# An adaptive-norm block on one core: the first tile's path to its first product, and the order around the fourth feed

## The reference, cut to what matters

```
u_m = u * mask                                # u: 64 x 64 x 1024, mask: position < length of the batch row
kernel[h, l] = 2 Re sum_n Cs[h, n] exp(dtA[h, n] * l)      # 64 heads h, 64 complex states n
y = causal_convolution(u_m, kernel) + u_m * D;  y = y * mask
scores = y @ Wr.T                             # 64 experts
gates = softmax(top 16 of scores), zero elsewhere
out = 2 * sum_k gates[k] * (y @ A[k].T) @ B[k].T           # rank 16 each
result = x + out
```

## Time and profile before

| | |
|---|---|
| median of 3 runs | 902.21 us (902.03 to 902.34) |
| the profiled execution | 900.6 us, its span 898.8 us |
| TensorE busy | 883.5 us, 98% of the span |
| VectorE busy | 764.9 us, 85% |
| ScalarE busy | 386.3 us, 43% |
| granted TensorE clock | 1.00 |

### The profile page before, as it was taken

How to read it: one execution, slowest core, us unless ns; L and a number is a source line. 1 busy time by engine, 2 the same in 40 slices (tenths; PEclk the granted TensorE clock), 3 DMA queues, 4 the chain that set the end, 5 groups by cost and what they waited for, 6 DMA issues and landing times.

```text
span 898.8 us, 15709 instructions
## 1 busy us (share of the span) xinstructions
PE 883.5 (98%) x4509; PEld 787.3 (88%) x4509; DVE 764.9 (85%) x2557; ACT 386.3 (43%) x682; POOL 2.0 (0%) x12
## 2 busy tenths in 40 slices
PE   5999999999999999999999999999999999999998
PEld 4667998998899998889998889998889999889997
DVE  8899989888898888898888898888888888888722
ACT  4763554344443354443344443344444344442100
POOL 0000000000000000000000000000000000000000
PEclk9999999999999999999999999999999999999999
DMA  6621214443434444434544333444433444344331
GB/s 221 253 58 47 77 30 135 112 125 105 116 103 111 125 120 105 109 105 106 134 111 111 107 112 96 134 111 111 109 120 100 120 111 113 109 123 107 99 94 47
DMA packets 67123, 99.85 MB, mean 111 GB/s; under 512 B 22944, under 2 KB 49184, under 8 KB 67104
## 3 DMA queue, kind: packets, MB, share of 16 engines
q1 hardware_dynamic: 66400, 99.16, 40.6%
q10 hardware_dynamic: 704, 0.46, 0.2%
HBM read 60.52 MB, written 34.87 MB: 106 GB/s over the span
## 4 chain that ended last, share of the span: by engine, by line
PE 93%; DVE 5%; ACT 1%; DMA 0%; issue 0%; ACTq 0%; DVEq 0%
PE out_ps L1286 25%; PE h_ps L1286 18%; PE out_ps L1290 12%; PE h_ps L1290 9%; PE turn_ps L1286 8%; PE turn_ps L1290 4%; PE conv_ps L1243 2%; PE conv_ps L1244 1%; PE conv_ps L1242 1%; PE conv_ps L1225 1%; PE conv_ps L1226 1%; PE conv_ps L1252 1%; PE conv_ps L1227 1%; PE conv_ps L1253 1%; PE conv_ps L1254 1%; PE h_ps L1295 1%
## 5 line engine op out<-in xcount | busy, mean ns | idle before, releaser
L1286 PE MATMUL out_ps<-b_lo,g_hi 128*128 128x512 f32 x496 | 195.3, 394 | 0.0
L1286 PE MATMUL out_ps<-b_hi,g_hi 128*128 128x512 f32 x496 | 195.2, 394 | 0.0
L1286 PE MATMUL h_ps<-a_hi,y_hi 128*128 128x384 f32 x480 | 161.4, 336 | 0.0
L1286 PE MATMUL h_ps<-a_lo,y_hi 128*128 128x384 f32 x480 | 161.3, 336 | 0.0
L1290 PE MATMUL out_ps<-b_hi,g_lo 128*128 128x512 f32 x496 | 122.9, 390 | 0.0
L1290 PEld LDWEIGHTS out_ps<-b_hi,g_lo 128*128 128x128 f32 x496 | 93.1, 188 | 20.3
L1286 PEld LDWEIGHTS out_ps<-b_hi,g_hi 128*128 128x128 f32 x496 | 93.1, 188 | 19.8
L1286 PEld LDWEIGHTS out_ps<-b_lo,g_hi 128*128 128x128 f32 x496 | 93.2, 188 | 19.5
L751 DVE SCALAR_TENSOR_TENSOR z<-swapped,step_other,part 128x64 f32<-128x64 f32 x384 | 92.3, 282 | 11.9
L744 DVE SCALAR_TENSOR_TENSOR part<-z,step_own,conv_ps 128x64 f32<-128x64 f32 x384 | 90.5, 277 | 8.5
L1290 PE MATMUL h_ps<-a_hi,y_lo 128*128 128x384 f32 x480 | 93.1, 336 | 0.0
(11 more groups left out here) (225 smaller groups left out, 1512.1 us busy)
## 6 DMA issues: line engine op xcount, KB each, us to landing
xt_in<-in_xt SPq DMA_DIRECT2D x32, 512.0 KB, 3.2
x_in<-in_x SPq DMA_DIRECT2D x62, 256.0 KB, 3.6
out<-x_in SPq DMA_DIRECT2D x62, 256.0 KB, 3.1
moved<-square_sb SPq DMA_DIRECT2D x28, 512.0 KB, 2.6
square_sb<-moved SPq DMA_DIRECT2D x112, 128.0 KB, 2.9
b_in<-in_b_t SPq DMA_DIRECT2D x8, 512.0 KB, 6.4
a_in<-in_a_t SPq DMA_DIRECT2D x8, 512.0 KB, 7.7
t_lo<-k_sb SPq DMA_DIRECT2D x62, 64.0 KB, 4.1
```

The source lines that it names most:

```text
L1286: pe.matmul(o, hi[:, c, :], moving[:, c, columns], start=first and c == order[0] and moving is w_hi, stop=False)
```

## The change

On the first tile:
- The parameters arrive by four transfers of 32 partitions (two per queue) instead of eight of 16. The first early block of B is loaded ahead of x, and ScalarE rounds it before its tanh instead of after the phases.
- `arguments(0)` moves ahead of the last weight operations. Two small operations make `weigh`, the real partitions' alpha and beta of the two heads.
- The kernel row comes straight from the powers: per head two products, with a column of `weigh` read 128 times (step 0) as weights. `out_factors(0)` goes behind `add_skip(0)`.
- TensorE starts with `whole_b(0)`, then 8 idle products instead of 14, then the row, and no longer waits for the rates. ScalarE's `low_weights(0)` stands ahead of `sines(0)`, and `copy_k(0)` ahead of `whole_in(0)`.
- The eight transfers of the block go out head by head with a semaphore for each. Near products run head by head; chunk 0 goes to a bank of its own and is masked alone, ahead of the third state step, then chunks 1 to 3 together. The mask itself is made in two halves, between the shuffle and the second part of two state steps. The from-states products of the upper chunks come before chunk 3's product with A instead of chunk 2's.

In the fourth iteration (t = 3) ScalarE takes the high part of the fed powers ahead of the y copies, and VectorE both `low_in` and `low_x` ahead of `low_row`.

```
-            for quad in range(P // QUAD):
-                first = quad * QUAD
-                sp.dma_start(par[first:first + PAIR, :, :], parameters[quad * PAIR:(quad + 1) * PAIR, :, :])...
-            sp.dma_start(xt_in[:, :, :], xt[0, :, :]).then_inc(s_xt, 16)
-            for i in EARLY:
-                load_weights(i)
+            for quad in (0, 1):
+                sp.dma_start(par[quad * QUAD:(quad + 1) * QUAD, :, :], states_of(quad)).then_inc(s_par, 16)
+            load_weights(EARLY[0])
+            sp.dma_start(xt_in[:, :, :], xt[0, :, :]).then_inc(s_xt, 16)
+            load_weights(EARLY[1])
...
-            for block, source in first_rows(0):
-                sp.dma_start(block, source).then_inc(s_t0, 16)
+            for i in range(HT):
+                for block, source in first_rows(i, range(0, JM // 2)):
+                    sp.dma_start(block, source).then_inc(s_t0[i], 16)
...      # ScalarE, start
+            split_weights(EARLY[0])
             act.wait_ge(s_rates, 1)
             act.activation(tanh_half[:, :], rates[:, :], ACT.Tanh, scale=0.5).then_inc(s_tanh, 1)
...
-            split_weights(EARLY[0])
+            low_weights(0)
             sines(0)
             split_weights(EARLY[1])
+            copy_k(0)
             whole_in(0, in_ps)
-            copy_k(0)
...      # ScalarE, step
+                second = isinstance(t, int) and t == LAGGED
                 if prep:
                     high_out(t + 2)
+                if second:
+                    high_in(t + 2)
                 if conv:
                     for i in range(HT):
                         high_y(t + 1, i)
                 if prep:
                     high_x(t + 2)
-                    if isinstance(t, int) and t == LAGGED:
-                        high_in(t + 2)
-                    else:
+                    if not second:
                         high_moved_in(t + 2)
...      # VectorE, start
+            arguments(0)
             dve.scalar_tensor_tensor(out=re_im, ...)
...
+            dve.tensor_scalar(weigh[:, 0, :], alpha[:, 0:HT], real_only[:, :], None, ALU.mult).then_inc(s_weigh, 1)
+            dve.tensor_scalar(weigh[:, 1, :], beta[:, 0:HT], real_only[:, :], None, ALU.mult).then_inc(s_weigh, 1)
             make_powers(0)
-            out_factors(0)
...
             add_skip(0)
+            out_factors(0)
...
-            states(0, range(1, 3))
-            ...                       # len_f and the whole mask
-            states(0, range(3, 4))
-            mask_first(0)
+            states(0, range(1, 2), lambda: mask_of(0, NC // 2))
+            states(0, range(2, 3), lambda: mask_of(NC // 2, NC))
+            dve.wait_ge(s_near0, 1)
+            dve.wait_ge(s_mask, 2)
+            mask_chunks(0, 1, s_ym0)
+            states(0, range(3, 4))
+            dve.wait_ge(s_conv0, HT)
+            mask_chunks(1, NC // 2, s_ym0)
             states(0, range(4, FED))
             arguments(1)
-            mask_first(1)
+            mask_chunks(NC // 2, NC, s_ym)
...      # VectorE, step
                 if prep:
                     low_out(t + 2)
+                    if second:
+                        low_in(t + 2)
+                        low_x(t + 2)
                     low_row(t + 2)
...
-                if prep:
+                if prep and not second:
                     low_x(t + 2)
-                    if second:
-                        low_in(t + 2)
-                    else:
-                        low_moved_in(t + 2)
+                    low_moved_in(t + 2)
...      # TensorE
+            def weighed_row():
+                pe.wait_ge(s_weigh, 2)
+                pe.wait_ge(s_powers, 1)
+                for i in range(HT):
+                    for part in range(2):
+                        last = pe.matmul(k_ps[:, i, :], weigh[:, part, i:i + 1].to_broadcast([P, P]), powers[:, i, part, 0:P], ...)
+                last.then_inc(s_kps, 1)
...
-            pe.wait_ge(s_rates, 1)
-            for n in range(14):
-                pe.matmul(turn_ps[:, 0, 0:P], ident[:, :], ident[:, :], start=True, stop=True)
             whole_b(0)
+            for n in range(8):
+                pe.matmul(h_ps[:, 0, 0:P], ident[:, :], ident[:, :], start=True, stop=True)
+            weighed_row()
             turn_in(0)
-            whole_row(0, k_ps)
             whole_feed(0)
-            pe.wait_ge(s_kcopy, 1)
             whole_b(1)
-            pe.wait_ge(s_t0, HT * JM * 16)
-            whole_near_0(0)
+            pe.wait_ge(s_blo, 2)
+            pe.wait_ge(s_t0[0], JM * 16)
+            whole_near_0(0, 0, 1)
+            whole_near_0(0, 1, NC // 2)
+            whole_near_0(0, NC // 2, NC)
+            pe.wait_ge(s_t0[1], JM * 16)
+            whole_near_0(1, 0, 1).then_inc(s_near0, 1)
+            whole_near_0(1, 1, NC // 2)
             whole_from_states_0(0)
-            whole_near_0(1).then_inc(s_near, 1)
+            whole_near_0(1, NC // 2, NC).then_inc(s_near, 1)
```

More of the change, by code:

```diff
@@ L475, in _ @@
             act.wait_ge(s_kdone, 1)
-            for block, source in first_rows(1):
-                act.dma_start(block, source).then_inc(s_t0, 16)
-            low_weights(0)
+            for i in range(HT):
+                for block, source in first_rows(i, range(JM // 2, JM)):
+                    act.dma_start(block, source).then_inc(s_t0[i], 16)
             theta(1)
@@ L734, in first_states, with mask_of, states @@
                 dve.wait_ge(s_first, HT * t + HT)
-            def states(t, chunks):
+            def mask_of(first, end):
+                dve.wait_ge(s_mask, 1)
+                dve.tensor_tensor(out=mask[:, first:end, :], in0=pos_f[:, first:end].unsqueeze(2).to_broadcast([P, end - first, B]),
+                                  in1=len_f[:, :].unsqueeze(1).to_broadcast([P, end - first, B]), op=ALU.is_lt).then_inc(s_mask, 1)
+            def states(t, chunks, amid=None):
                 n, moves = HT * t, FED - 1
@@ L1227, in feed @@
                     pe.matmul(fed, in_lo[:, i, :], xt_hi[:, i, 0:NS], start=False, stop=True).then_inc(s_fed, 1)
+            def weighed_row():
+                pe.wait_ge(s_weigh, 2)
+                pe.wait_ge(s_powers, 1)
+                for i in range(HT):
+                    for part in range(2):
+                        last = pe.matmul(k_ps[:, i, :], weigh[:, part, i:i + 1].to_broadcast([P, P]), powers[:, i, part, 0:P],
+                                         start=part == 0, stop=part == 1)
+                last.then_inc(s_kps, 1)
             def whole_feed(t, heads=range(HT)):
@@ L1254, in from_states, with whole_near_0 @@
                     pe.matmul(later, o_lo[:, i, 1:P + 1], z_hi[:, :, i, :], start=False, stop=True).then_inc(s_conv, 1)
-            def whole_near_0(n):
-                columns = slice(n * HALF // 2, (n + 1) * HALF // 2)
-                for i in range(HT):
-                    last = pe.matmul(conv_0[n][:, i, :, :], t_lo[:, i, :].bitcast(F32), xt_in[:, i, columns],
-                                     start=i == 0, stop=False, skip_group_check=True)
-                return last
+            def whole_near_0(i, first, end):
+                n = first // (NC // 2)
+                target = first_conv[:, i, :] if end == 1 else conv_0[n][:, i, first - n * (NC // 2):end - n * (NC // 2), :]
+                return pe.matmul(target, t_lo[:, i, :].bitcast(F32), xt_in[:, i, first * B:end * B],
+                                 start=i == 0, stop=end == 1 and i == HT - 1, skip_group_check=True)
             def whole_from_states_0(n):
```

55 lines of the change are left out of this document (30 added, 25 removed).

## The result

| | before | after |
|---|---|---|
| median | 902.12 us (900.73 to 902.34, 4 runs) | 912.43 us (911.07 to 913.26, 4 runs) |
| ratio | | 1.0121, 95% interval 1.0109 to 1.0132 |
| profiled execution, its span | 900.6, 898.8 us | 911.1, 909.3 us |
| mean granted clock | 1.00 | 0.994 |

I had forecast 902.6 with 900.7 to 904.1 as range. The prediction was wrong.

The account below looks back on a forecast made before the run. VectorE was taken to set the pace up to 151 us, TensorE being full after 153. First tile -1.1 plus fourth iteration +1.55 gave +0.45 on 900.6; with 1.6 to the median, 902.6 us, range 900.7 to 904.1.

Parts of the forecast that it names:

- Parameters: First tile's start: two transfers per queue instead of four let VectorE start sooner; gain 0.87 us (bounds 0.5 and 0.95).
- ScalarE's copy ahead of the tanh: First tile: copy waits for the 512 KB load landing at 4.85; table load ends at 7.2, cover missing by 0.1 us.
- a microsecond later: First tile: if the 512 KB load lands a microsecond later, all behind it is a microsecond later.
- Arguments, powers, row, block: First tile: arguments and powers gain 1.05 us, the row's transfers issue 1.7 sooner, head 1 begins at 20.95, gain 1.4.
- Masks and states: First tile: TensorE's first product 2.6 us sooner, at 22.6, but VectorE's fourth state step only 1.1 sooner, at 23.75.
- -1.1: First tile's total: 1.1 us sooner (bounds -2.2 and +0.2).
- The fourth iteration: VectorE idles 1.7 us for x's high part; feed wait shrinks, new waits come in the fifth iteration; +1.55 us (-0.6 to +2.2).
- Rival C, the clock: TensorE falls to its slow rate between dummies and row; 3 to 5 us on top of 902.6; chance 0.10.
- the constant of 1.6: Whole kernel: the median shown, 902.21, lies 1.6 us above the profiled execution; the same difference is added to the forecast.
- A: First product and fourth iteration's feed: each TensorE wait that goes is gained, 2.6 and 1.6 us; 898.0; chance 0.06.
- B: First tile -1.1 as worked out, fourth iteration neutral or better, 0 to -0.6; 900.5 to 901.1 us; chance 0.14.
- D: First load lands a microsecond or more late, the first tile gains nothing; 903.4 to 904.2 us; chance 0.10.

Follow-up runs that it names:

- Run 1: Kernel before, only the parameters by four transfers with a two-level source (2 groups of 16 rows), two per queue; 908.49 us, ratio 1.0085.
- run 3: Changed kernel, host lays parameters out in partition order so each transfer reads one block of 48 KB; 902.37 us, ratio 1.0007.
- Run 14: Changed kernel with the fourth iteration put back to its old order, source still 2 slabs of 16 rows, 96 KB apart; 910.65 us.
- 9 to 16: Parameter source written as two levels over one block, or in 16, 8, 4 or 2 slabs at varied distances, on run 4's kernel or Run 14; 899.97 to 911.03 us.
- run 9: run 4's kernel with the same contiguous parameter bytes written as 2 by 16 rows; 901.12 us, ratio 0.9990.
- run 2: Kernel before with only the fourth iteration's new order on ScalarE and VectorE; 903.54 us, ratio 1.0028.
- run 5: run 3 with ten idle products on TensorE ahead of near in the fifth iteration; 900.95 us, ratio 0.9996.
- run 4: Changed kernel with parameters laid out flat by the host and the old order of the fourth iteration; 899.88 us, ratio 0.9985.
- run 7: Changed kernel, parameters still late, with 18 idle products ahead of the row instead of 8; 911.28 us, ratio 1.0116.
- 18: Kernel before with only eight idle products on TensorE ahead of the fourth iteration's feed; 900.82 us, ratio 0.9994.

## Why the prediction was wrong, point by point

**The failed step** is the first, *Parameters*: "Gain 0.87 (bounds: 0.5, if the two-level pattern costs more to issue; 0.95)". I priced the transfer by its bytes and its issue. Measured: 9.46 against the forecast 3.15, and 4.02 before, so a loss of 5.4 us; the issue of two takes 1.95 us where 0.92 was expected. Experiments 1, 3 and 14 pin it on the source alone, 9 to 16 on its two slabs. The mean of the changed kernel is 912.30, with the flat source 902.18: 10.1 us for the layout of one source. With it flat the parameters come at 3.36, a gain of 0.66.

The Trainium skill's page "DMA: Bandwidth & Descriptors" (Why a DMA increments its semaphore by 16 and not by 1) states the rule that I overlooked: the engines of a transfer are the largest number up to 16 that divides the slowest dimension of both sides, as the instruction carries it. The runs agree: 2, 4, 8, 16 slabs land at 9.5 to 11.0, 6.6, 4.4, 4.2 us, and 2 by 16 over one block (run 9), which need not be carried as two levels, at 3.5. That 16 slabs come later than one block, which would have 16 engines as well, the rule does not say. With it "the parameters land late" would have been the likeliest case and not a bound of 0.37 us, though no row of before gave its price.

**ScalarE's copy ahead of the tanh**: the order was no trap, but by two errors that cancel. With the flat source the copy comes at 5.96 (forecast 4.85), 1.1 late; and the table load, which I had put between copy and tanh, stands ahead of both (1.68 to 2.96), so the tanh comes 1.36 behind the copy's start, at 7.32 (7.2). In the changed kernel it comes at 10.03, because the 512 KB load is behind the slow transfers. The bound "a microsecond later" was too near, for the same cause.

**Arguments, powers, row, block**: right in their lengths. Relative to the parameters the powers come 0.27 sooner than before (10.31 behind them instead of 10.58). Flat, they end at 14.5 (14.25), the row takes 1.13 (1.2), so columns read 128 times are loaded like others. Head 1 (21.17, forecast 20.95) and the first product (22.80, 22.6) are within 0.25 us. But the 22.36 that I set against head 1 is where head 0's near begins in the kernel before; like against like, near begins at 20.18 instead of 22.36. The sum did not use that gain of 1.4.

**Masks and states**: right. With the flat source and the old feed TensorE's wait for VectorE ends 1.0 sooner (50.70 for 51.72) against -1.1; the 2.4 us that TensorE is ahead at the first product do not reach VectorE. (The terms in the text, 17.8, 0.2 and 5.9, make 23.9 and not 23.75 for the fourth step; it came at 23.52.)

**The fourth iteration**: right in its mechanism. VectorE in the changed kernel, 140 to 147:

```profile
140.22 1.23 DVE L736 TENSOR_TENSOR xt_lo<-xt_in,xt_hi 128x1024 fp32r<-128x1024 f32 x1 [1.28 <-ACT xt_hi L461]
...
146.56 0.70 DVE L669 TENSOR_TENSOR powers<-turned,decay 128x520 f32<-128x520 f32 x1 [0.49 <-ACT decay L411]
```

It stands still 1.28 us (forecast 1.7) for x's high part, the powers wait 0.49 for ScalarE (0.45), and the iteration costs 1.2 in the changed kernel and 1.26 in run 2 (1.55). What failed is that a new wait of 3 us was booked at its length alone: the clock behind it costs 1.5 more where it falls, 1.2 at the mean (run 5).

**Rival C, the clock** had a chance of 0.10, its place was named rightly (between the idle products and the row), its cause was not: the gap is 2.5 us only because the parameters are late. Its price: the same matmuls from the row to head 1 of near take 9.39 us in the changed kernel and 6.64 in run 3 at full clock, 2.75 more. The rest of the difference is the parameters: they are 6.1 later (9.46 and 3.36), and the wait for VectorE's state step ends 8.8 later (59.45 and 50.65). Run 14 against run 4 gives 2.4 in the same way (9.02 and 6.64; 9.96 later there, the parameters 7.6). Run 1 has its parameters 6.1 late without a fall, and its span is 6.1 longer. So the price is 2.4 to 2.75 us, under the 3 to 5 that I had given; run 7 took half of it away.

I had argued that "idles of 1.3 and 1.8 us are followed by fast matmuls". That was one execution: the median shown, 902.21, lay 1.6 above the profiled one, and I carried that difference along as a constant. It was the same wait of 1.8 us with a fall of the clock behind it (18). So the nearness of run 3 to the forecast is partly luck: the constant of 1.6 holds the fall behind the old feed's wait, which run 3 no longer has, and the fall behind its new wait, which I had not booked, has taken its place. Without falls (5 against 18) the whole change with a flat source costs 0.13 at the mean, against +0.45. The Trainium skill's page "TensorE: Matmul & The Clock Gate" (What's actually happening) lets the array fall to 1.2 GHz after idling; the runs agree (0.50 behind the waits of 2.49 and 2.78 us), and add that behind a wait of 1.8 us it happens in some executions only (11 of 27).

**Rivals A, B and D**: A fell, no TensorE wait was gained as such. B's first half is run 4; its second, a neutral fourth iteration, fell with run 2. D had the late load; what came late was the parameters, and the load behind them.

## What to carry to other kernels

Before pieces of a transfer are joined, look at the slowest dimension that is left on each side once adjoining levels are taken together: with 2 there the joined transfers landed 5.4 us after their halves here. Lay the source out flat on the host, or cut it so that 16 stands outermost, which here made the parameters 0.8 to 1.2 us later than flat. And where the median of the runs lies apart from the profiled execution, look at each run's clock: a wait of about 2 us at TensorE may cost 1.5 us beside its length, and the eight idle products put into it here took that away for 0.1 us or less.

## What the runs showed of the hardware that was not expected

- Transfers of 48 KB from two slabs each stand in the changed kernel's chain of waits (start, duration) with 7.39 us, the last line below; from one block each they land 1.8 and 2.1 us after issue. They hold up what is issued behind them: x lands 8.5 us after its issue, against 5.7 and 5.1 in 3 and 4.
- A source with gaps costs issue time on its own: 0.80 us for each transfer of 16 slabs on ScalarE's queue, 0.98 to 1.03 of 2 to 8, against 0.45 of one block.
- TensorE's clock can fall after work has begun again: in run 4 it idles until 136.19, is at 1.00 until 137, then at 0.57 on the mean of 4 us. It can also fall before it: in the changed kernel shortly before 20.60. In the profiles kept, the wait before the first product left aside, a fall came with every wait of 2.5 to 5.4 us and with none of up to 1.5; of the waits of 1.8 to 2.2 us, nine had one and five had none.

```profile
2.05 7.39 DMA par<-in_parameters
```
